# Attention of a decoder layer: row maxima and softmax bias in three fused vector passes, and the attention levels transposed in two DMAs

## The reference, cut to what matters

```
q, k = _fq_sym(q, axis=-1), _fq_sym(k, axis=-1)      # 8-bit levels x a step per row
v = _fq_sym(v, axis=2)
attn = softmax(q @ k.T)                              # over 2048 keys
attn = _fq_unsigned(attn, axis=-1)                   # round(attn / (max/255)) * (max/255)
out  = attn @ v
```

## Time and profile before

| | us |
|---|---|
| median of 3 runs (lowest, highest) | 2473.56 (2473.38, 2480.1) |
| the profiled execution's own time | 2477.05 |
| its span, first to last instruction | 2475.3 |
| busy: PE / DVE / ACT / POOL | 1950.7 / 1785.8 / 1634.9 / 501.7 |
| attention, first to last bias instruction | 1328.57 to 2226.51 |

### The profile page before, as it was taken

One profiled execution on the slowest core, in us unless ns is written; L12 is line 12 of the kernel. 1 busy time (PEld: TensorE's weight loads), 2 busy tenths in 40 slices (PEclk: granted clock), 3 DMA queues, 4 the chain that ended last, 5 costly groups with the idle time before them and its releaser, 6 DMA issues. The chain is left out here.

```text
span 2475.3 us, 42289 instructions
## 1 busy us (share of the span) xinstructions
PE 1950.7 (79%) x12019; PEld 1265.1 (51%) x12084; DVE 1785.8 (72%) x2918; ACT 1634.9 (66%) x2564; POOL 501.7 (20%) x410
## 2 busy tenths in 40 slices
PE   5886999999999999995466776767767677773698
PEld 4664878777787877773353222222222222223587
DVE  4996676777767687775646888888888888885333
ACT  3775888888888888881436767677676767772111
POOL 0000555555555555550000000000000000001000
PEclk9997999999999999997876555555555555556799
DMA  1002000000000000001004878778777877881000
GB/s 57 17 8 86 0 26 0 25 0 25 25 0 25 0 25 0 25 0 49 7 0 77 153 146 149 147 148 149 146 148 147 149 148 147 149 155 52 18 17 17
DMA packets 558402, 164.84 MB, mean 67 GB/s; under 512 B 535073, under 2 KB 550817, under 8 KB 558369
## 3 DMA queue, kind: packets, MB, share of 16 engines
q1 hardware_dynamic: 558368, 164.44, 33.4%
HBM read 28.09 MB, written 2.10 MB: 12 GB/s over the span
## 5 line engine op out<-in xcount | busy, mean ns | idle before, releaser
L1222 ACT ACTIVATE levels<-s_ps,nb,qstep 128x1024 int16<-128x1024 f32 x512 | 612.2, 1199 | 267.6 <-DVE nb L1180 267.6
L1170 DVE TENSOR_REDUCE mx<-s_ps 128x1 f32<-128x512 f32 (+1 forms) x768 | 659.5, 865 | 98.3 <-PE s_ps L1115 81.5
L1115 PE MATMUL s_ps<-kT,qT 48*128 48x512 bf16 x1024 | 521.9, 612 | 264.5 <-ACT levels L1222 262.6
L588 DVE SCALAR_TENSOR_TENSOR xs<-x_ps,cw,xs 128x508 f32<-128x508 f32 (+2 forms) x393 | 291.3, 741 | 174.8 <-ACT xs L510 137.4
L1115 PEld LDWEIGHTS s_ps<-kT,qT 48*128 (+1 forms) x1024 | 82.4, 104 | 514.3 <-issue 490.9
L479 PE MATMUL o_ps<-wo,hid 128*128 x1024 | 243.0, 380 | 4.7 <-DVE acc L575 4.7
L644 POOL TENSOR_TENSOR hid<-y,sg 128x512 f32<-128x512 f32 x128 | 175.4, 1370 | 278.6 <-ACT sg L532 185.8
L1125 PEld LDWEIGHTS ao_ps<-vi,levels_T 128*128 128x128 f16 x4096 | 129.5, 105 | 185.2 <-issue 185.2
L1340 POOL TENSOR_TENSOR o_rstd<-o_mv,o_minus_half 128x16 f32<-128x16 f32 x1 | 2.9, 2902 | 1037.7 <-DVE o_mv L902 1037.7
L479 PEld LDWEIGHTS o_ps<-wo,hid 128*128 128x128 f32 x1024 | 192.6, 189 | 40.2 <-issue 9.8
L510 ACT ACTIVATE xs<-x_ps,cb,cw 128x512 f32<-128x512 f32 x131 | 101.9, 778 | 116.9 <-PE x_ps L431 116.9
(11 more groups left out here) (195 smaller groups left out, 3356.3 us busy)
## 6 DMA issues: line engine op xcount, KB each, us to landing
w_raw<-winT_dram SPq DMA_DIRECT2D x18, 512.0 KB, 4.5
wo_raw<-woutT_dram SPq DMA_DIRECT2D x9, 512.0 KB, 5.6
levels_T<-levels SPq DMA_TRANSPOSE x256, 4.3
w_bc<-winT_dram SPq DMA_DIRECT2D x18, 128.0 KB, 2.2
xT<-xT_dram SPq DMA_DIRECT2D x4, 512.0 KB, 7.9
acc<-x_dram SPq DMA_DIRECT2D x1, 2048.0 KB, 11.0
ctxT<-ctxT_dram SPq DMA_DIRECT2D x4, 512.0 KB, 7.5
out_dram<-f_out SPq DMA_DIRECT2D x16, 128.0 KB, 1.7
```

The lines of the kernel that those rows point to most:

```text
L588: dve.scalar_tensor_tensor(to, x_ps[:, :, 0:SEQ - s], cw[:, head, TAPS - 1 - s], to, ALU.mult, ALU.add).then_inc(chain if s < TAPS - 1 els ...
L1115: return pe.matmul(s_ps[:, BANKS[h % 2][chunk], :], qT[:, bass.ds(round_, 1), h % NH, :].rearrange("p b t -> p (b t)"), kT[:, h % NH, at:a ...
L1170: dve.tensor_reduce(mx[:, h % 2, at:at + 1], src, AX.XY if what == "cd" else AX.X, ALU.max).then_inc(max_chain, 1)
L1222: act.activation(levels[:, s, half * HALF:(half + 1) * HALF].rearrange("p (c k) -> p c k", c=2), s_ps[:, first:first + 2, :], ACT.Exp, bia ...
```

## The change

Three things are edited, all in `attention`.

1. The three TENSOR_REDUCE and the two bias instructions of a unit are replaced by three `tensor_tensor_reduce` (`lowest`). Each computes (score + shift) * (-step) element by element, writes it in bf16 to a scratch tile `spill`, and accumulates the minimum, starting from an initial value, into a [128,1] output. With shift = ln 255 / (-step) the element is ln 255 - step*score, and its minimum over the row is nb. The minimum of b (started from 3e38) starts c,d, whose minimum starts a, whose minimum is nb. So c,d waits for b, a for c,d, and b for the a of the unit before (they share `spill`). The scale, and for c,d and a the initial value, are per-partition operands in SBUF; the shift is a [128,1] value broadcast along the row.
2. `nstep` and `shift` now hold one query tile only. `steps` makes them in three small DVE instructions at h = 15 of each tile, ahead of chunk b of the next one. `sums` is kept for two tiles in place of 16. PE's wait for `nstep` at the start is gone.
3. SP issues two DMA transposes per unit, of 128x1024 levels each: the first after `ab_exp`, the second after `cd_exp`. Both count on the same semaphore `turned`, so PE and ACT wait for 32 in place of 16 per unit.

```diff
@@ sync
-                    sp.wait_ge(cd_exp, n + 1)
-                    if exists(qt, h, -RING):
+                    for half, written in enumerate((ab_exp, cd_exp)):
+                        sp.wait_ge(written, n + 1)
+                        if half == 0 and exists(qt, h, -RING):
+                            sp.sem_inc(held, 1)
+                            sp.wait_ge(pv_done, n + (1 - RING))
                         sp.sem_inc(held, 1)
-                        sp.wait_ge(pv_done, n + (1 - RING))
-                    sp.sem_inc(held, 1)
-                    sp.dma_start_transpose(lT[:, s, :, :].bitcast(F16), levels[:, s, :].bitcast(F16)).then_inc(turned[s], 16)
+                        tiles = slice(half * (HALF // P), (half + 1) * (HALF // P))
+                        sp.dma_start_transpose(lT[:, s, tiles, :].bitcast(F16),
+                                               levels[:, s, half * HALF:(half + 1) * HALF].bitcast(F16)
+                                               ).then_inc(turned[s], 16)
@@ vector
+            def lowest(n, h, what):
+                u = h % 2
+                bank = BANKS[u]
+                ready, first, banks, init, to, done = {
+                    "b": (b_ready, bank["b"], 1, 3.0e38, low[:, u, 0:1], low_chain),
+                    "cd": (cd_ready, bank["c"], 2, low[:, u, 0:1], low[:, u, 1:2], low_chain),
+                    "a": (a_ready, bank["a"], 1, low[:, u, 1:2], nb[:, u:u + 1], nb_ready)}[what]
                 dve.wait_ge(ready, n + 1)
-                dve.tensor_reduce(mx[:, h % 2, at:at + 1], src, AX.XY if what == "cd" else AX.X,
-                                  ALU.max).then_inc(max_chain, 1)
...
+                if what != "b":
+                    dve.sem_inc(held, 1)
+                    dve.wait_ge(low_chain, n * 2 + (1 if what == "cd" else 2))
+                elif not (isinstance(n, int) and n == 0):
+                    dve.sem_inc(held, 1)
+                    dve.wait_ge(nb_ready, n)
+                dve.sem_inc(held, 1)
+                dve.tensor_tensor_reduce(spill[:, 0:banks * GT],
+                                         s_ps[:, first:first + banks, :].rearrange("p c k -> p (c k)"),
+                                         shift[:, h % NH:h % NH + 1].to_broadcast([P, banks * GT]),
+                                         nstep[:, h % NH:h % NH + 1], init,
+                                         ALU.add, ALU.min, to).then_inc(done, 1)
+            def steps(at):
+                if not (isinstance(at, int) and at == 0):
+                    dve.wait_ge(nb_ready, at * NH)
+                    dve.sem_inc(held, 1)
+                dve.tensor_scalar(nstep[:, :], qstep[:, bass.ds(at, 1), :].rearrange("p q h -> p (q h)"),
+                                  -1.0, None, ALU.mult).then_inc(step_chain, 1)
+                dve.wait_ge(step_chain, at * 3 + 1)
+                dve.sem_inc(held, 1)
+                dve.reciprocal(shift[:, :], nstep[:, :]).then_inc(step_chain, 1)
+                dve.wait_ge(step_chain, at * 3 + 2)
+                dve.sem_inc(held, 1)
+                dve.tensor_scalar(shift[:, :], shift[:, :], LN255, None, ALU.mult).then_inc(step_chain, 1)
+                dve.wait_ge(step_chain, at * 3 + 3)
+                dve.sem_inc(held, 1)
@@ body
+                    if h == NH - 1 and exists(qt, h, 1):
+                        steps(qt + 1)
                     if exists(qt, h, 1):
-                        maxima(n + 1, h + 1, "b")
+                        lowest(n + 1, h + 1, "b")
                     if h == LAG and exists(qt, 0, -1):
                         finish(qt, qt - 1)
                     if exists(qt, h, 1):
-                        maxima(n + 1, h + 1, "cd")
-                        maxima(n + 1, h + 1, "a")
-                        bias(n + 1, qt if h < NH - 1 else qt + 1, h + 1)
+                        lowest(n + 1, h + 1, "cd")
+                        lowest(n + 1, h + 1, "a")
```

More of the change, by code:

```diff
@@ L1064, in sem @@
             return ctx.enter_context(nc.semaphore(name))
-        mx = sb("mx", [P, 2, 3])
-        mall = sb("mall", [P, 2])
+        low = sb("low", [P, 2, 2])
         nb = sb("nb", [P, 2])
-        nstep = sb("nstep", [P, BATCH, NH])
+        shift = sb("shift", [P, NH])
+        spill = sb("spill", [P, HALF], BF16)
+        nstep = sb("nstep", [P, NH])
         levels = sb("levels", [P, RING, T], I16)
         lT = sb("levels_T", [P, RING, T // P, P], I16)
-        sums = sb("sums", [P, BATCH, NH, 2])
+        sums = sb("sums", [P, 2, NH, 2])
         tot = sb("tot", [P, NH])
@@ L1076, in attention @@
         o_ps = ctx.enter_context(nc.psum_tensor("ao_ps", [P, GT], F32))
-        consts, a_ready, b_ready, cd_ready, max_chain, nb_ready, ab_exp, cd_exp, pv_done, scaled, chain = (
-            sem("at_" + n) for n in ("consts", "a_ready", "b_ready", "cd_ready", "max_chain", "nb_ready", "ab_exp",
+        step_chain, a_ready, b_ready, cd_ready, low_chain, nb_ready, ab_exp, cd_exp, pv_done, scaled, chain = (
+            sem("at_" + n) for n in ("step_chain", "a_ready", "b_ready", "cd_ready", "low_chain", "nb_ready", "ab_exp",
                                      "cd_exp", "pv_done", "scaled", "chain"))
@@ L1121, in values @@
                 s = h % RING
-                pe.wait_ge(turned[s], qt * (16 * NH // RING) + (h // RING + 1) * 16)
+                pe.wait_ge(turned[s], qt * (32 * NH // RING) + (h // RING + 1) * 32)
                 pe.sem_inc(held, 1)
@@ L1147, in body @@
                         score(qt, h + 2, "d").then_inc(cd_ready, 1)
-            pe.wait_ge(consts, 1)
             score(0, 0, "b").then_inc(b_ready, 1)
@@ L1162, in _ @@
         def _(dve):
[L1163 to L1168, removed]
-                dve.wait_ge(ready, n + 1)
-                dve.tensor_reduce(mx[:, h % 2, at:at + 1], src, AX.XY if what == "cd" else AX.X,
-                                  ALU.max).then_inc(max_chain, 1)
@@ L1173, in bias @@
[L1173 to L1181, removed]
+            def lowest(n, h, what):
[5 more added lines that the diff above has]
+                    "a": (a_ready, bank["a"], 1, low[:, u, 1:2], nb[:, u:u + 1], nb_ready)}[what]
+                dve.wait_ge(ready, n + 1)
+                if what != "b":
[10 more added lines that the diff above has]
+                                         ALU.add, ALU.min, to).then_inc(done, 1)
@@ L1183, in finish @@
             def finish(qt, last):
-                both = sums[:, bass.ds(last, 1), :, :].rearrange("p q h s -> p (q h) s")
+                both = sums[:, bass.ds(last % 2, 1), :, :].rearrange("p q h s -> p (q h) s")
                 dve.wait_ge(pv_done, last * NH + NH)
@@ L1202, in body @@
                     if exists(qt, h, 1):
-                        maxima(n + 1, h + 1, "cd")
-                        maxima(n + 1, h + 1, "a")
-                        bias(n + 1, qt if h < NH - 1 else qt + 1, h + 1)
[L1207 to L1212, removed]
+                        lowest(n + 1, h + 1, "cd")
+                        lowest(n + 1, h + 1, "a")
+            steps(0)
+            lowest(0, 0, "b")
+            lowest(0, 0, "cd")
+            lowest(0, 0, "a")
             rounds(dve, body)
@@ L1223, in exps @@
                                ACT.Exp, bias=nb[:, u:u + 1], scale=qstep[:, bass.ds(qt, 1), h],
-                               accum_out=sums[:, bass.ds(qt, 1), h, half:half + 1].rearrange("p q s -> p (q s)")
+                               accum_out=sums[:, bass.ds(qt % 2, 1), h, half:half + 1].rearrange("p q s -> p (q s)")
                                ).then_inc(cd_exp if half else ab_exp, 1)
@@ L1231, in body @@
                     if exists(qt, h, -RING):
-                        act.wait_ge(turned[h % RING], qt * (16 * NH // RING) + h // RING * 16)
+                        act.wait_ge(turned[h % RING], qt * (32 * NH // RING) + h // RING * 32)
                     exps(n, qt, h, 0)
```

## The result

The changed kernel takes 2508.75 us (median of 4 runs, 2500.1 to 2509.57) beside 2474.32 for the kernel before in the same comparison (4 runs, 2473.38 to 2480.1). The ratio is 1.0126, 95% interval 1.0099 to 1.0153: slower by 1.3%, where 2514 (1.6%) was forecast. The profiled executions have spans of 2506.8 and 2475.3 us, a difference of 31.5.

A forecast was written before the change was run, and what follows sets the result against it. Before, a dependence loop of 3.49 us bound attention (901.4 us); after, DVE's turn: 2.876 + 0.24 + 0.45 = 3.57. 256 x 3.57 + 29 = 943, about +40, so 2514 us on the median's scale (1.6% slower), range 2425 to 2600.

The forecast's parts named there:

- The mechanism: Attention loop: mall, nb and gaps (0.59 us) leave; DVE's chained passes become the bound at 3.57 us per unit.
- Length of a pass: DVE's three fused passes: b 738, c,d 1341, a 797 ns, with 59 per per-partition operand; sum 2.876 us.
- the rival of half the rate: DVE passes stream at half rate: 2.13 us more per unit, about +590, 3060 us; chance 0.03.
- Writing the minimum out: Each DVE pass pays 0.08 us for its accumulator output, 0.24 per unit; bounds nothing and 0.19.
- the first rival: DVE's three passes: the minimum costs nothing to write, DVE's turn 3.33, 2454 us, faster; chance 0.22.
- The gaps: Wait ahead of each DVE pass, riding on a held instruction: 0.15 us, three per unit, 0.45.
- The mark that the forecast set itself: Forecast is wrong if DVE's three passes sum to under 2.95 us with what they write.
- Once per tile: DVE's steps adds 1.06 us and finish 0.90 per tile, all counting: 15 x 1.96 = 29 us.
- Ends: Attention's start: steps(0) adds 0.6 us; its end: a shorter last transpose gives about -1; together nothing.
- Two transposes: SP issues two halves in 2.3 us per unit, up to 2.7: hidden under 3.57.
- the DMA rival: DMA engines full from smaller reads: at half as much packet time again 4.2 us per unit, +174, 2650 us; chance 0.05.
- the rival loops: Loops through DVE, ACT and PE: short one 3.09 us, one spanning two units 3.33 each, both below DVE's 3.57.

The follow-up runs named there:

- b free: Changed kernel, but b's pass writes to its own part of spill and doesn't wait for the previous unit's a; c,d takes that wait: 2499.17 us, ratio 1.008.
- no chain: Changed kernel, but passes start from constants with own scratch and wait for no pass right before; minima of b and c,d left out: 2446.79 us, ratio 0.9862.
- two waits: As b free, but a's scratch is a row of att, so no pass has more than two waits: 2488.14 us, ratio 1.0038.
- c and d first: As two waits, but PE makes c and d of unit n+2 ahead of the values of n-3: 2483.57 us, ratio 1.0019.
- lighter steps: As c and d first, but reciprocals made once for all tiles and steps is two small instructions with one wait: 2477.98 us, ratio 1.0001.

## Why the prediction was right, point by point

*The mechanism* was right. The reading it starts from holds: no engine is full in the earlier trace rows, and the loop of dependences in the earlier trace rows is as long as the distance of two exponentials there, 3.49. mall and nb left the loop, the three chained passes on DVE became the bound, PE and ACT wait for it; taking the chain away (each second wait is then for a pass long done) gives 62 us back (2509 to 2447), taking the split away gives nothing. DVE is 82.6% busy, and three gaps of 0.19 in 3.63 us are another 15.7%: 98% busy or held, over the 95% foreseen.

*Length of a pass.* Forecast 738, 1341 and 797; measured 751, 1344 and 810, a sum of 2.905 for 2.876. The 59 ns per per-partition operand, read from a [128,256] instruction, holds: 810 - 751 = 59. The time per element stayed: (1223 - 687)/512 = 1.05 ns before, (1344 - 810)/512 = 1.04 after. So the rival of half the rate, 2048 x 1.05 = 2.14 us more per unit by these rows, falls.

*Writing the minimum out.* Forecast 0.08 per pass, and here the step failed: there is a read instruction of its own behind each pass, and it is 0.083 long. But it overlaps its pass and adds some 0.015. The premise of the first rival, that the minimum costs nothing to write, was nearly true.

*The gaps.* Forecast 0.15, measured 0.19. Taken together the two are 0.23 against 0.20 per pass, and the unit is 3.50 rather than 3.57. This second error is why the rival lost in spite of its premise: with write-outs at nothing and gaps of 0.15 it had 3.33; with 0.20 from pass to pass it is 2.905 + 0.60 = 3.50. The gap after the small instructions in `steps` is 0.15, as in the earlier trace rows; the 0.04 more stands ahead of a fused pass: it starts 0.15 behind the start of its `sem_inc`'s record, the small instructions of `steps` and of the earlier trace rows 0.11. The mark that the forecast set itself, three passes under 2.95 with what they write, lies exactly on what was measured (2.905 + 3 x 0.015).

*Luck.* The way the time moved, and how near it came, rest in part on two errors of opposite sign. With the write-out at its 0.015 and the gaps still at the forecast's 0.15, the same sum has 2.876 + 0.045 + 0.45 = 3.37 per unit, and 256 x 3.37 + 29 - 901.4 = -10: a kernel that is 0.4% faster. The place was foreseen, and that a link of the chain costs about 0.2; that it would be the wait and not the write-out was not.

*Once per tile.* Forecast 1.06 for `steps` and 0.90 for `finish`, 1.96 together; measured 1.42 and 0.73, 2.15 (2.25 by the total). `steps` was short by its last gap, 0.48 in place of 0.15: behind the last small instruction stand a wait with computed value for it, and two more of the pass. That these waits make the difference is not shown. `finish` was less, because the gap that it fills was counted on top of it.

*Sum.* 255 x (3.50 - 3.57) = -18 and 15 x 0.29 = +4 make 28 of the forecast 41.5; the 3.3 us of other code's difference bring the profile to 31.5. *Ends:* +0.5 and -0.75 for +0.6 and -1.

*Two transposes.* Hidden, at 2.47 us of issue per unit for the 2.3 (up to 2.7) worked out; SP waits 178.4 us in 234 units, 0.76 each. The halves don't load the DMA engines more, so the DMA rival falls: 0.80 of 3.52 and 0.75 of 3.63 us are 2.8 and 2.7 per unit. With the split alone the share is 0.79 beside 0.80 and the time the same. In the first rival the two-unit loop without write-outs is (6.65 - 0.16) / 2 = 3.25, not equal to DVE's 3.33, which doesn't change its time.

*What the forecast didn't see*, and what recurs in five expectations behind it that were too low (b free, no chain, two waits, c and d first, and lighter steps, which was counted from the one before): it priced the rival loops (3.09 and 3.33) with the hand-over of 0.11 from the kernel before. With two or three waits ahead of the pass it is 0.30 to 0.50; with it the short loop is 3.37 and the two-unit loop 3.48, just under DVE's turn. Freeing DVE alone thus gains little before they bind.

*Not settled:* why a wait on a minimum starts the next pass 0.19 us late, and why two waits for the same value take 0.37 where one takes 0.11. The 0.11 is from the kernel before, where the wait rides on the instruction itself; here each wait rides on a `held` instruction ahead of another kind of pass. The runs price an unsatisfied wait, arithmetic between two waits and a third wait, but they don't part the second wait from the `held` instructions: the one fused pass with a single wait, b from "two waits" on, doesn't wait for PE in the steady units. Nor was it tried to make the waits of `steps` the same way, or to join the fixed address of -step with the split transposes.

## What to carry to other kernels

Count an accumulating DVE pass as it came out here: a plain one (0.69 us for 128x512, 1.22 for 128x1024) plus 59 ns per per-partition operand, and 0.2 us more only if the next instruction waits for it; a fusion that turns independent passes into a chain pays that at each link: 3 x 0.2 here, as much as the 0.59 that leaving out two small instructions and their gaps saved. When a loop's bound moves, price the next loops with the waits that the changed code has, not with those of the old one. And before fusing, look at the small instructions themselves: a [128,1] operand at a fixed address, in place of one whose address is computed behind the wait, made this kernel 0.7% faster.

## What was unexpected of the hardware

- An accumulator read of 0.083 us on DVE runs under the last 0.07 of its pass.
- A [128,1] operand whose address is computed in a register, by an addition on which the wait rides (0.04 us), costs 0.10 us there (0.13 to 0.03).
- The hand-over of PE to DVE. To a: 0.11 with one wait on the instruction itself, 0.37 with two waits in a row, 0.45 with a register addition between the two. To c,d: 0.30 with two waits in a row, 0.38 to 0.48 with arithmetic between them, 0.50 with three waits and arithmetic.
- A wait that is long satisfied still costs some 0.11 us when it stands behind the one that comes last (gap of 0.31 in place of 0.20).
- The issue of a DMA transpose grows less than its size: 1.92 us for 128x2048, 1.23 for 128x1024.
